# The tail of a one-core Trainium2 kernel: pairs of batches on halves of the TensorE array

## The reference

```
# end of the Mamba block: y is 1101 x 128 per batch
h1  = y @ W_out.T                                   # out-projection, 128 -> 64
h1  = leaky_relu(h1 @ W_ff1.T + b_ff1)
h   = h + sigmoid(h1 @ W_ff2.T + b_ff2)
# last block, on x = layernorm(h)
weights = x @ wr + br                               # the router: one number per token
idx     = top_k(weights, 550)[:549]                 # the selected tokens
y       = gelu(x[idx] @ w1 + b1) @ w2 + b2          # 64 -> 256 -> 64
out     = h + x + scatter(idx, y * weights[idx])
```

## Time and profile before

| | us |
|---|---|
| median of 3 runs (1128.1 to 1129.8) | 1129.52 |
| profiled execution, its own time | 1129.4 |
| its span, first to last recorded instruction | 1127.6 |

### The profile page before, as it was taken

The page is one execution under the profiler, slowest core; times in us unless marked ns, Lnnn a source line. Parts: engine busy times, 40 slices in busy tenths (PEclk is TensorE's granted clock), DMA queues, the critical chain, the costliest instruction groups (busy, mean ns, idle before and its releaser), DMA issues.

```text
span 1127.6 us, 11525 instructions
## 1 busy us (share of the span) xinstructions
PE 834.5 (74%) x3813; PEld 356.0 (32%) x3813; DVE 807.0 (72%) x1046; ACT 516.2 (46%) x1014; POOL 554.8 (49%) x357
## 2 busy tenths in 40 slices
PE   5588045577786699787688777878788788878887
PEld 3244022364673333343111111111112111114466
DVE  0223779976653333337799999999999999994365
ACT  0137141018425266554455555555555444544621
POOL 0000646753010000001399999999999999981100
PEclk8799568668756599998567878765765766669876
DMA  9900000070010000000111001100110110000001
GB/s 224 183 1 1 0 1 0 0 164 1 1 56 1 1 1 1 0 1 19 25 38 41 25 17 41 41 21 20 41 36 14 32 41 22 19 1 1 1 15 27
DMA packets 28248, 33.08 MB, mean 29 GB/s; under 512 B 10142, under 2 KB 27550, under 8 KB 27678
## 3 DMA queue, kind: packets, MB, share of 16 engines
q1 hardware_dynamic: 28190, 32.36, 12.9%
HBM read 17.57 MB, written 1.20 MB: 17 GB/s over the span
## 4 chain that ended last, share of the span: by engine, by line
PE 35%; DVE 32%; issue 13%; ACT 12%; POOL 3%; SPq 2%; DMA 2%; DVEq 0%; ACTq 0%; POOLq 0%
DVE pair_arrays L1577 14%; ACT pair_arrays L897 5%; DVE pair_arrays L1561 4%; PE PS L750 3%; PE PS L732 3%; ACT PS L897 3%; PE PS L722 3%; PE PS L576 3%; PE PS L842 2%; PE PS L512 2%; DMA big<-in_x 2%; DVE pair_arrays L1383 2%; SPq L360 2%; PE PS L483 2%; PE PS L868 2%
## 5 line engine op out<-in xcount | busy, mean ns | idle before, releaser
L1241 POOL TENSOR_TENSOR pair_arrays<-pair_arrays 128x736 f32<-128x736 f32 x192 | 331.7, 1743 | 21.4 <-DVE pair_arrays L1577 21.0
L897 ACT ACTIVATE PS<-PS,A_negative 128x368 f32<-128x368 f32 x384 | 191.4, 538 | 128.3 <-PE PS L732 127.6
L1577 DVE TENSOR_TENSOR_SCAN pair_arrays<-PS,scan_carry,pair_arrays 128x368 f32<-128x368 f32 x256 | 235.7, 962 | 0.7 <-ACT PS L897 0.4
L1203 POOL TENSOR_TENSOR big<-pair_arrays 128x1104 f32<-128x1104 f32 (+15 forms) x32 | 60.5, 1910 | 154.4 <-DVE pair_arrays L1337 118.6
L1561 DVE TENSOR_TENSOR pair_arrays<-pair_arrays,PS 128x736 f32<-128x736 f32 x144 | 128.7, 894 | 5.9 <-PE PS L722 5.7
L750 PE MATMUL PS<-pair_arrays,weights 128*32 128x368 f32 x768 | 130.1, 680 | 2.9 <-POOL pair_arrays L1241 2.9
L1577 DVE TENSOR_TENSOR_SCAN pair_arrays<-PS,pair_arrays 128x368 f32<-128x368 f32 x128 | 110.0, 904 | 0.7 <-ACT PS L897 0.5
L1249 POOL TENSOR_TENSOR pair_arrays<-pair_arrays,token_weights 128x736 f32<-128x736 f32 x48 | 83.9, 1748 | 23.9 <-DVE big L1539 23.9
L722 PE MATMUL PS<-spread_rows,token_weights 96*128 96x368 bf16 x192 | 62.1, 414 | 39.2 <-DVE pair_arrays L1561 28.6
L722 PE MATMUL PS<-pair_arrays,token_weights 96*128 96x368 bf16 x192 | 67.3, 445 | 28.8 <-DVE pair_arrays L1561 22.5
L1262 POOL TENSOR_TENSOR pair_arrays<-big 128x368 f32<-128x368 f32 x24 | 18.6, 796 | 136.6 <-PE PS L652 136.6
(11 more groups left out here) (190 smaller groups left out, 1277.3 us busy)
## 6 DMA issues: line engine op xcount, KB each, us to landing
big<-in_x SPq DMA_DIRECT2D x8, 1024.0 KB, 21.2
big<-decay_rows SPq DMA_DIRECT2D x4, 1104.0 KB, 15.1
spread_rows<-pair_arrays SPq DMA_DIRECT2D x96, 46.0 KB, 1.9
pair_arrays<-pair_arrays SPq DMA_DIRECT2D x96, 46.0 KB, 1.9
spread_rows<-big SPq DMA_DIRECT2D x48, 46.0 KB, 1.9
pair_arrays<-big SPq DMA_DIRECT2D x48, 46.0 KB, 1.9
weights<-in_wts SPq DMA_DIRECT2D x1, 2204.0 KB, 22.3
big<-in_wexp SPq DMA_DIRECT2D x1, 1536.0 KB, 7.8
```

What stands on the lines that cost most here:

```text
L897: return nc.scalar.activation(o, i, fn, **kw)
L1203: nc.gpsimd.tensor_tensor(prod[n % 4][:, 0:NC * (L - lag)].rearrange("p (c r) -> p c r", r=L - lag), chunks(q_[:, p, :])[:, :, lag:L], chu ...
L1241: nc.gpsimd.tensor_tensor(hcbuf[t % NRING], hbuf[t % NRING], c4(seg).unsqueeze(1).to_broadcast([128, 2, G]), ALU.mult).then_inc(s("hc_read ...
L1577: nc.vector.tensor_tensor_scan(hbuf[t % NRING][:, h, :], PS[:, 4 + 2 * (t % 2) + h, 0:G], bx[t % NRING][:, h, :], carry[:, a:a + 1] if k e ...
```

## The change

The order of stages stays. Four things differ.

- Out-projection: the two batches' matmuls use 64 of the array's columns each (batch 0 writes partitions 0 to 63 of the bank, batch 1 partitions 64 to 127), without accumulation.
- Router rows: `weight_rows` takes a pair. Two matmuls with 64 rows each, on the two halves of the array, write two neighbouring banks, and one ACT operation of 2x368 columns evicts both. There are 6 pairs of banks' worth instead of 12 single ones, and the columns of batch 0 now come before the rows of pair 1.
- First layer: `hidden(p, y)` does the same for a pair. It always writes banks 4 and 5, so each call after the first waits for the GELU of the call before (`hid_ready` m; before it was m - 1), and one GELU of 2x368 columns serves both. The 12 calls stand in batches 0 (pair 0) and 1 (pair 1); batches 2 and 3 have none.
- `rows_out`, `residual_rows`, and the waits of DVE count pairs.

```diff
--- before.py
+++ after.py
@@ -772,8 +772,9 @@
                     if g >= 2:
                         pe.wait_ge(s("mo_ev"), g - 1)
                     for b2 in range(2):
-                        last = nc.tensor.matmul(PS[:, g % 2, 0:G], w("WoutT")[:, b2 * 128:(b2 + 1) * 128],
-                                                batch_array(3, 2 * p + b2)[:, cols(k)], start=(b2 == 0), stop=(b2 == 1))
+                        last = nc.tensor.matmul(PS[half(b2), g % 2, 0:G], w("WoutT")[:, b2 * 192:b2 * 192 + 64],
+                                                batch_array(3, 2 * p + b2)[:, cols(k)], start=True, stop=True,
+                                                skip_group_check=True)
                     last.then_inc(s("mo_ps"), 1)
                 if 1 <= g <= NGR:
                     p, k = groups[g - 1]
@@ -797,16 +798,18 @@
 
             pe.wait_ge(s("ln_out"), 4 * NGR)
 
-            def weight_rows(b):
+            def weight_rows(p):
                 for k in range(NG):
-                    m = b * NG + k
+                    m = p * NG + k
                     if m >= 2:
                         pe.wait_ge(s("wrow_ev"), m - 1)
-                    nc.tensor.matmul(PS[:, m % 2, 0:G], w("wr")[:, (b % 2) * 128:(b % 2 + 1) * 128], P1[:, b // 2, cols(k)],
-                                     start=True, stop=True).then_inc(s("wrow_ps"), 1)
+                    for b2 in range(2):
+                        last = nc.tensor.matmul(PS[:, 4 * (m % 2) + b2, 0:G], w("wr")[64 * b2:64 * b2 + 64, b2 * 128:(b2 + 1) * 128],
+                                                P1[64 * b2:64 * b2 + 64, p, cols(k)], start=True, stop=True)
+                    last.then_inc(s("wrow_ps"), 1)
 
             def weight_columns(b):
-                pe.wait_ge(s("wrow_ev"), NG * (b + 1))
+                pe.wait_ge(s("wrow_ev"), NG * (b // 2 + 1))
                 if b:
                     pe.wait_ge(s("wcol_ev"), b)
                 for j in range(NT):
@@ -816,17 +819,18 @@
                 last.then_inc(s("wcol_ps"), 1)
 
             weight_rows(0)
+            weight_columns(0)
+            weight_rows(1)
             for b in range(1, B):
-                weight_rows(b)
-                weight_columns(b - 1)
-            weight_columns(B - 1)
+                weight_columns(b)
 
             def fill(b):
 
 
                 steps = [[] for _ in range(NT)]
-                for y in range(2 * NG):
-                    steps[y].append((hidden, (b, y)))
+                if b < NPAIR:
+                    for y in range(2 * NG):
+                        steps[y].append((hidden, (b, y)))
                 if b == 0:
                     for i in range(len(RESID)):
                         steps[i + 1].append((residual_rows, (i,)))
@@ -835,17 +839,20 @@
                     steps[4].append((rows_out, (2 * (b - 1) + 1,)))
                 return steps
 
-            def hidden(b, y):
-                m = b * 2 * NG + y
-                if m >= 2:
-                    pe.wait_ge(s("hid_ready"), m - 1)
-                nc.tensor.matmul(PS[:, 4 + m % 2, 0:G], w("w1")[:, (b % 2) * HF + (y // NG) * 128:(b % 2) * HF + (y // NG + 1) * 128],
-                                 P1[:, b // 2, cols(y % NG)], start=True, stop=True).then_inc(s("hid_ps"), 1)
+            def hidden(p, y):
+                m = p * 2 * NG + y
+                if m:
+                    pe.wait_ge(s("hid_ready"), m)
+                for b2 in range(2):
+                    a = b2 * HF + (y // NG) * 128
+                    last = nc.tensor.matmul(PS[:, 4 + b2, 0:G], w("w1")[64 * b2:64 * b2 + 64, a:a + 128],
+                                            P1[64 * b2:64 * b2 + 64, p, cols(y % NG)], start=True, stop=True)
+                last.then_inc(s("hid_ps"), 1)
 
             def residual_rows(i):
                 pr, j0, nj, n = RESID[i]
                 pe.wait_ge(s("residual"), 1)
-                pe.wait_ge(s("wrow_ev"), B * NG)
+                pe.wait_ge(s("wrow_ev"), NPAIR * NG)
                 if i >= 2:
                     pe.wait_ge(s("resid_ev"), i - 1)
                 for j in range(nj):
@@ -856,7 +863,7 @@
             def rows_out(x_):
 
                 n, members = ROWS[x_]
-                pe.wait_ge(s("hid_ready"), (members[-1][0] + 1) * 2 * NG)
+                pe.wait_ge(s("hid_ready"), (members[-1][0] // 2 + 1) * 2 * NG)
                 if x_ < 2:
                     pe.wait_ge(s("wcol_ev"), B)
                     pe.wait_ge(s("resid_ev"), len(RESID))
@@ -1150,14 +1157,18 @@
                 f(wcol[:, b, 0:NT - 1], PS[:, 2, b * NT:b * NT + NT - 1], ACT.Copy)
                 f(wcol[0:LAST, b, NT - 1:NT], PS[0:LAST, 2, b * NT + NT - 1:b * NT + NT], ACT.Copy).then_inc(s("wcol_ev"), 1)
 
-            for b in range(B):
+            def weight_rows(p):
                 for k in range(NG):
-                    m = b * NG + k
+                    m = p * NG + k
                     act.wait_ge(s("wrow_ps"), m + 1)
-                    f(wrow[b][:, cols(k)], PS[:, m % 2, 0:G], ACT.Identity, bias=col("br")).then_inc(s("wrow_ev"), 1)
-                if b:
-                    weight_columns(b - 1)
-            weight_columns(B - 1)
+                    f((P5, P6)[p][:, :, cols(k)], PS[:, 4 * (m % 2):4 * (m % 2) + 2, 0:G], ACT.Identity,
+                      bias=col("br")).then_inc(s("wrow_ev"), 1)
+
+            weight_rows(0)
+            weight_columns(0)
+            weight_rows(1)
+            for b in range(1, B):
+                weight_columns(b)
 
             def residual_part(i):
                 pr, j0, nj, n = RESID[i]
@@ -1165,15 +1176,14 @@
                 f(RES[0:n, 2 * pr:2 * pr + 2, j0:j0 + nj, :].rearrange("q b j d -> q j b d"),
                   PS[0:n, i % 2, 0:nj * 128].rearrange("q (j b d) -> q j b d", j=nj, b=2), ACT.Copy).then_inc(s("resid_ev"), 1)
 
-            for b in range(B):
+            for p in range(NPAIR):
                 for y in range(2 * NG):
-                    m = b * 2 * NG + y
-                    act.wait_ge(s("hid_ps"), m + 1)
-                    f(hid[b][:, y // NG, cols(y % NG)], PS[:, 4 + m % 2, 0:G], ACT.Gelu_apprx_tanh,
+                    act.wait_ge(s("hid_ps"), p * 2 * NG + y + 1)
+                    f(pool_[:, 6 + 2 * p:8 + 2 * p, y // NG, cols(y % NG)], PS[:, 4:6, 0:G], ACT.Gelu_apprx_tanh,
                       bias=col("b1a" if y < NG else "b1b")).then_inc(s("hid_ready"), 1)
-                    if b == 0 and y:
+                    if p == 0 and y:
                         residual_part(y - 1)
-                if b == 0:
+                if p == 0:
                     residual_part(len(RESID) - 1)
 
 
@@ -1651,7 +1661,7 @@
 
             for b in range(B):
                 dve.wait_ge(s("wcol_ev"), b + 1)
-                dve.wait_ge(s("wrow_ev"), NG * (b + 1))
+                dve.wait_ge(s("wrow_ev"), NG * (b // 2 + 1))
                 for j in range(NT):
                     t0, n = j * 128, (128 if j < NT - 1 else LAST)
                     x_ = b * NT + j
```

## The result

The changed kernel takes 1138.44 us (median of 4 runs, 1137.42 to 1139.36), the kernel before 1128.81 (median of 4). The ratio is 1.008, 95% interval 1.0052 to 1.0108. The prediction was 1138. Executions more than 1.5% above the fastest of their kernel are in the medians and left out of the ratios.

What follows compares the result with a forecast made beforehand. PE carries the tail and its granted clock is the main term. -2.15 - 0.65 + 6.9 + 10.2 - 6.3 + 0.6 = +8.6 us on 1129.4 gives 1138; range 1125 to 1143.

Steps and rivals of the forecast that it cites:

- A pair of halves: PE's half-array matmuls: four instructions of 64 rows need 0.82 us until the next piece, 0.20 of it for the shape change.
- Part 1: Out-projection: 0.21 us less in each of 4 rounds and 1.3 less in the first two groups, -2.15 us.
- Part 2: Router rows: 14.15 us before, 14.1 at the low clock, 11.2 at the high; taken as 13.5, -0.65 us.
- Part 3: Batch 0: pairs now wait for the previous GELU; 16 us against 9.1, +6.9 us (bounds +2.9, +7.9).
- Part 4: Batch 1: 22.3 us at the low clock, 14.6 at the high; taken as 21.5, +10.2 us.
- a sign: Named as showing the forecast right: PE waits for the GELU before first-layer pairs, 0.7 to 1 us each.
- Part 5: Batches 2 and 3, without first layer, at the low clock: 12.0 us (-6.3) and 23.6 us (+0.6).
- Sum: All parts of the tail together: +8.6 us on the profiled execution's 1129.4, giving 1138.
- Rival A: The clock follows PE's busy share and the tail runs at 1.00: -9.9 us, 1119.5; chance 0.09.
- Rival B: Clock high in batches 0 and 1, low after: -3.1 us, 1126.3; chance 0.13.
- Rival C: Clock high in batch 0 and part of batch 1: +0.4 us, 1129.8, no change; chance 0.10.
- Rival D: The halves do not overlap in the tail, each pair costing 2.9 us at the low clock: 1152; chance 0.02.

Runs made afterwards that it cites:

- e3: The kernel before with the first layer's change alone (pairs in batches 0 and 1, one pair of banks): median 1142.06 us, ratio 1.0101.
- e4: The changed kernel with 25 unread full-width fp32 matmuls added where PE waits: median 1126.05 us, ratio 0.9974 against the kernel before.
- e6: The changed kernel with 25 fillers as in e4, each made of 24 single-column bf16 matmuls instead: median 1147.62 us, ratio 1.0138.
- e8: The changed kernel, without fillers, with two pairs of banks for the first layer instead of one: median 1132.91 us, ratio 1.0022.
- e5: The kernel before with two unread full-width matmuls ahead of PE's first wait in batches 1 to 3: median 1118.64 us, ratio 0.9914.
- e1: The kernel before with the out-projection's change alone: median 1132.46 us, ratio 0.9989.
- e2: The kernel before with the router rows' change alone: median 1130.89 us, ratio 0.9997.
- e7: The kernel of e4 with pair 1's six first-layer calls spread over batches 1 and 2: median 1124.47 us, ratio 0.9952 against the kernel before.
- e9: e5 plus the changed out-projection and router rows, and two fillers ahead of batch 3's last count: median 1114.5 us, ratio 0.9867.

## Why the prediction was right

The forecast, the mechanism and its size hold: the clock is low through almost all of batches 1 to 3, and this goes with the streams that the change takes away (e3 brings it about, e4 undoes it, e6 does not, and e8 keeps it although its pairs no longer wait). The prediction sees one side less well: it holds the change against the kernel before as it is, partly at the low level. By its own high-clock figures (12.0, 14.6, 11.0 and 17.9 us for the four batches) against e5's (7.5, 11.3, 11.2 and 19.8), the new first layer would lose some 6 us at the high level too. Point by point:

- **A pair of halves.** Predicted 0.82 us to the next piece, because the change of shape costs 0.20. Measured 0.77 (1027.39 to 1028.16), and 2.20 for a round against 2.26. The Trainium skill, "TensorEngine Tiling (Array Packing)", Key Properties, has the drain at a change of mode; 0.77 where halving gives 0.62 agrees.
- **Part 1, -2.15.** Right as the price of the edit (2.2 at either level, e1 and the stages above) and not seen in the profiled pair, because the changed kernel began the stage at 0.50 (until 1025.8) and the kernel before at 1.00. The step was sized from one profile, whose starting level I took as given.
- **Part 2, -0.65.** 11.3 to 11.5 us in the profiles that ran more than half of the stage at the high level (e2, e4, e6, e7, e9; predicted 11.2 for all of it) and 14.4 at the low one (predicted 14.1). I took 13.5, a mixture; the profile was low all through. The low level also slows the single-column transposes, 1.52 us from one batch's columns to the next against 1.14, which I had left at the high clock's price.
- **Part 3, +6.9 against +4.6.** The mis-sized term. I had 16 us for batch 0; it took 13.7, since the clock came back at 1073.6 in the middle of it. In e3 it didn't, and batch 0 took 16.4. The bounds 12.0 and 17.0 held both. The prediction says that the clock before was at 1.00 until 1084.5; it was low in the first 3.4 us of batch 0 (1064.1 to 1067.5), so the 9.1 us it starts from are a mixture too.
- **Part 4, +10.2 against +9.3.** 20.6 us, for the reason given: the first two pairs ran high, the rest low (e3, all low: 22.1 against 22.3 worked out). The waits for the GELU were 0.29 to 0.71 us, where 0.7 to 1 had been named as a sign.
- **Part 5.** Batch 2 12.1 against 12.0. The last three `rows_out` took 3.05 each and not 3.3 (9.14 for 48): -0.1 instead of +0.6. The 3.3 was the distance to the next piece behind a single call; three calls in a row cost less each.
- **Sum.** +8.2 in the tail against +8.6. That it is so close is luck: parts 1 and 2 came out 3.5 us dearer than predicted, parts 3, 4 and 5 together 3.8 cheaper, and they cancel. The median agrees to 0.4 us with 1.4 us from upstream in it.

Rival A, that the clock follows PE's busy share, is refuted by e6; its -1.5 for part 2 also does not fit its own 11.2 against 14.15, which gives -2.95 and some 1118. The Trainium skill, "TensorE: Matmul & The Clock Gate", Part 1, says that activity releases the throttle; read as PE's busy time, the traces do not bear it out (96% busy at the low level in e6). Rival B needed the high level in batch 1, which it had for 4.4 us only. Rival C is the nearest: batch 0 was high for 5.8 us and batch 1 for 4.4, at +13.9 for the two instead of its +8.9. Rival D (no overlap of halves) is refuted by the 0.77 us.

## What to carry to other kernels

Before you shorten TensorE's work, ask what the clock will do: here a first layer on halves of the array, with half the streaming and one pair of banks, made the kernel 1% slower (e3). Read the granted clock by stretches and look at what PE did just ahead of each fall. Filling three gaps of 1.2 to 1.4 us with matmuls that nobody reads made the kernel before 10 us faster. When you judge a change by its clock, feed the kernel that you compare it with as well. Merging two consumers into one operation over two banks halves the buffering, so count the chain from one producer to the next before the evictions saved.

## What the runs showed that I had not expected

- The kernel before could be had 10 us faster by adding work (e5), and 1.3% faster with the change's out-projection and router rows added to it (e9). The fastest kernel of the series is the one that leaves the first layer as it was.
- The level at which a stage starts differs from execution to execution. It goes with 2.5 us in the out-projection stage, and the level in the router stage with 3. Single runs of the kernel before went from 1122.8 to 1140.6 us, so one profile of it gives a stage's time only for the level that it happened to have.
